# A vision block in ten token tiles of 128 rows instead of eleven of 111

## What is computed

```python
h = concat([cls, patches @ W.T + b], 1) + pos_enc          # 32 x 37 x 256, patches of 768 values
# mixer, on x = layernorm(h); cumsum runs over the tokens of one image
Z   = cumsum(x, 1) / counts                                 # counts = 1..37
a_b, a_t = (x @ Wq.T) @ V_b, (x @ Wq.T) @ V_t
c_b, c_t = cumsum((x @ Wk.T) @ W_b, 1), cumsum((x @ Wk.T) @ W_t, 1)
out = (a_b * c_b @ U_b.T + alpha * (a_t * (Z @ X_t) * c_t @ U_t.T)) / counts + bias
h   = h + out @ Wo.T
# experts, on x = layernorm(h): 8 experts, 256 -> 1024 -> 256, gelu, best two by softmax(x @ w_router + b_router)
# expert e takes its first 185 tokens in token order (cap), the rest of its tokens get nothing from it
h   = h + sum over kept choices of gate * expert_e(x) / sum of kept gates
```

## Time and profile before

| what | value |
|---|---|
| median of three runs | 164.17 us |
| profiled execution | 163.18 us |
| its span | 161.4 us |
| mean granted clock of TensorE | 0.993 |
| instructions | 3080 |

### The profile page before, as it was taken

The page is one execution under the profiler, slowest core; times in us unless marked ns, Lnnn a source line. Parts: engine busy times, 40 slices in busy tenths (PEclk is TensorE's granted clock), DMA queues, the critical chain, the costliest instruction groups (busy, mean ns, idle before and its releaser), DMA issues.

```text
span 161.4 us, 3080 instructions
## 1 busy us (share of the span) xinstructions
PE 152.6 (95%) x1033; PEld 143.7 (89%) x1033; DVE 105.6 (65%) x342; ACT 83.0 (51%) x208; POOL 53.3 (33%) x54
## 2 busy tenths in 40 slices
PE   7999999999999999989899999999999999999950
PEld 7669999978799799889889989999999999999950
DVE  0085983598477898994098858769488596694610
ACT  4125653482256979434335658366573774746200
POOL 3003550007140000121717427266183580703351
PEclk9999999999999999999999999999999999999997
DMA  5999960088005444300189985897879878710422
GB/s 174 403 418 415 403 196 0 2 295 276 0 0 140 120 131 133 85 4 0 52 255 350 314 276 84 300 262 247 254 138 314 261 203 258 177 19 4 47 24 23
DMA packets 17263, 28.47 MB, mean 176 GB/s; under 512 B 1289, under 2 KB 13875, under 8 KB 17125
## 3 DMA queue, kind: packets, MB, share of 16 engines
q1 hardware_dynamic: 14789, 25.48, 46.9%
q0 software_dynamic: 2464, 2.86, 10.3%
HBM read 24.20 MB, written 4.14 MB: 176 GB/s over the span
## 4 chain that ended last, share of the span: by engine, by line
PE 76%; DMA 10%; DVE 3%; issue 3%; POOL 2%; SPq 1%; POOLq 1%; ACT 1%; DVEq 0%
PE ps L1265 21%; PE ps L1288 10%; PE ps L1114 7%; PE ps L1169 7%; DMA w_even<-w 5%; PE ps L1094 5%; PE ps L1184 4%; PE ps L1290 4%; DMA first_t<-first 4%; PE ps L1199 3%; PE ps L1226 2%; PE ps L1298 2%; PE ps L1204 2%; DMA rows_in<-xrows,src_row 2%; PE ps L1212 1%
## 5 line engine op out<-in xcount | busy, mean ns | idle before, releaser
L498 POOL DMA_INDIRECT out_rows<-out_s,dst_row x16 | 23.8, 1486 | 38.6 <-ACT out_s L664 32.2
L640 ACT ACTIVATE first_t<-ps,b_cur 128x186 f32<-128x186 f32 x64 | 23.1, 413 | 24.7 <-PE ps L1265 24.7
L1288 PE MATMUL ps<-hid_hl,split 128*128 128x372 f32 x96 | 29.0, 369 | 0.0
L1290 PE MATMUL ps<-hid_hl,split 128*128 128x186 f32 x96 | 23.9, 249 | 0.0
L1265 PE MATMUL ps<-first_t,w_even 128*128 128x186 f32 x128 | 21.8, 322 | 0.7 <-ACT first_t L525 0.7
L1265 PE MATMUL ps<-first_t,patch_t 128*128 128x186 f32 x128 | 21.7, 322 | 0.1
L964 DVE CAST hid_hl<-first_t 128x372 fp32r<-128x372 f32 x28 | 10.9, 388 | 15.7 <-ACT first_t L640 15.7
L1265 PEld LDWEIGHTS ps<-first_t,w_even 128*128 128x128 f32 x128 | 20.1, 190 | 1.0 <-issue 1.0
L1265 PEld LDWEIGHTS ps<-first_t,patch_t 128*128 128x128 f32 x128 | 20.1, 190 | 0.4 <-issue 0.4
L483 POOL DMA_INDIRECT rows_in<-xrows,src_row x14 | 15.4, 1097 | 10.5 <-DVE src_row L934 6.5
L1290 PEld LDWEIGHTS ps<-hid_hl,split 128*128 128x128 f32 x96 | 18.3, 191 | 0.0
(11 more groups left out here) (173 smaller groups left out, 286.0 us busy)
## 6 DMA issues: line engine op xcount, KB each, us to landing
w_even<-w SPq DMA_DIRECT2D x8, 1024.0 KB, 5.8
patch_t<-w SPq DMA_DIRECT2D x8, 1024.0 KB, 5.4
patch_t<-patches SPq DMA_DIRECT2D x2, 972.0 KB, 11.7
att<-attn SPq DMA_DIRECT2D x1, 1280.0 KB, 8.9
first_t<-first SPq DMA_DIRECT2D x1, 870.0 KB, 6.5
out_rows<-h SPq DMA_DIRECT2D x3, 288.0 KB
xrows<-xn SPq DMA_DIRECT2D x3, 288.0 KB, 2.4
first_t<-first SPq DMA_DIRECT2D x1, 580.0 KB, 4.2
```

What stands on the lines that cost most here:

```text
L498: pool.indirect_dma_start(out=out[:, :], out_offset=bass.IndirectOffsetOnAxis(ap=dst_row[0:SIZES[s], c:c + 1], axis=0), in_=out_s[q][0:SIZ ...
L640: ins = act.activation(hid[:, f, :], bank(pair)[:, (f % 2) * SL:(f % 2 + 1) * SL], ACT.Gelu, bias=b1_cur[q][:, f:f + 1])
L1288: pe.matmul(dst[:, 0:2 * SL], w2_h[q][:, f, cols], hid_hl[:, f].rearrange("p a s -> p (a s)"), start=f == 0, stop=False)
L1290: ins = pe.matmul(dst[:, 0:SL], w2_l[q][:, f, cols], hid_hl[:, f, 0], start=False, stop=f == KF - 1)
```

## The change

Tiles have 128 rows, so ten of them, the last with 32; groups have 2, 3, 3 and 2 tiles. Group edges no longer fall between images: a group's patches are those of the images that its tokens reach (7, 11, 10 and 4 images instead of 9, 9, 9 and 5), and the scans start from the last column of the group before. POOL scales from a table spread over all images. `means2` goes from DVE to ACT, the router's bias is added in `rstd2`, `choose` loses its own bias, reduction and flooring ahead of the maximum. The marks carry the row in the tile, the tile's first row and a one for "taken", three parts instead of two, and `read_marks` sums the first two in one reduction. Four bridge products in front of `slots 0` go, two come in front of `slots 1`. The orders of all engines are written anew: A goes before B_ from `xn_t` on.

```diff
-TB = 3
-TT = TB * T
+TT = 128
-GROUPS = [(0, 3), (3, 3), (6, 3), (9, 2)]
+GROUPS = [(0, 2), (2, 3), (5, 3), (8, 2)]
-BRIDGES = {('slots', 0): 4, ('pick', 0): 3}
+BRIDGES = {('pick', 0): 3, ('slots', 1): 2}
-CHOICES = [(0, 6), (6, 5)]
-PATCHES = [(t0 * TB, min(B, (t0 + n) * TB)) for t0, n in GROUPS]
+CHOICES = [(0, 5), (5, 5)]
+ENDS = [0] + [min(B, -(-(t0 + n) * TT // T)) for t0, n in GROUPS]
+PATCHES = list(zip(ENDS[:-1], ENDS[1:]))
...
-    c[:, C_IDS] = np.stack([p + 1 + 0 * t, 0 * p + t], -1).reshape(128, -1)
+    c[:, C_IDS] = np.stack([p + 0 * t, 0 * p + t * TT, 1 + 0 * p + 0 * t], -1).reshape(128, -1)
...
-        UNITS = [("proj", A, 0), ("mac", 0, 1), ("uw", 0, 2), ("proj", B_, 3), ("norm1", A, 0), ("proj", C, 1),
-                 ("norm1", B_, 2), ("proj", E, 3), ("norm1", C, 0), ("xn_t", B_, 1), ("norm1", E, 2), ("xn_t", A, 3),
-                 ("zc", B_, 1), ("zc", A, 3), ("a", A, 0), ("a", B_, 2), ("xn_t", E, 1), ("xn_t", C, 3), ("y", B_, 2),
-                 ("zc", C, 1), ("norm2", B_, 3), ("y", A, 0), ("a", E, 2), ("zc", E, 1), ("norm2", A, 0), ("a", C, 1),
-                 ("y", E, 3), ("y", C, 2), ("norm2", E, 1), ("norm2", C, 3), ("slots", 0, 2), ("pick", 0, 0),
-                 ("slots", 1, 2), ("pick", 1, 0)]
+        UNITS = [("proj", A, 0), ("mac", 0, 1), ("uw", 0, 2), ("norm1", A, 0), ("proj", B_, 3), ("proj", C, 1),
+                 ("norm1", B_, 2), ("xn_t", A, 3), ("norm1", C, 0), ("proj", E, 1), ("xn_t", B_, 3), ("zc", A, 2),
+                 ("zc", B_, 1), ("a", B_, 3), ("norm1", E, 0), ("a", A, 2), ("xn_t", C, 1), ("y", A, 2), ("zc", C, 1),
+                 ("y", B_, 2), ("xn_t", E, 3), ("norm2", A, 0), ("zc", E, 3), ("norm2", B_, 1), ("a", E, 2), ("a", C, 3),
+                 ("y", E, 0), ("y", C, 2), ("norm2", E, 3), ("norm2", C, 0), ("slots", 0, 2), ("pick", 0, 1),
+                 ("slots", 1, 2), ("pick", 1, 1)]
...
         DVE_ORDER = [("proj", A), ("uw", 0), ("stats1", A), ("proj", B_), ("rstd1", A), ("proj", C), ("stats1", B_),
...
+                     ("xn_low", A), ("rstd1", B_), ("stats1", C), ("rstd1", C), ("proj", E), ("sums", A), ("sums", B_),
+                     ("prod", A), ("stats1", E), ("add_up", A), ("prod", B_), ("rstd1", E), ("sums", C), ("add_up", B_),
+                     ("sums", E), ("rstd2", A), ("prod", E), ("prod", C), ("add_up", E), ("rstd2", B_), ("add_up", C),
+                     ("choose", 0), ("rstd2", E), ("place", 0), ("count", 0), ("rstd2", C), ("choose", 1), ("below", 0),
+                     ("place", 1), ("count", 1), ("know", 0), ("know", 1)]
+        ACT_ORDER = [("mac", 0), ("m_high", 0), ("root1", A), ("norm1", A), ("xn_high", A), ("root1", B_), ("norm1", B_),
+                     ("root1", C), ("xn_copy", B_), ("norm1", C), ("xn_copy", C), ("root1", E), ("norm1", E), ("xn_copy", E),
+                     ("means2", A), ("squares2", A), ("keep2", A), ("root2", A), ("rows2", A), ("means2", B_),
+                     ("squares2", B_), ("root2", B_), ("keep2", B_), ("rows2", B_), ("means2", E), ("squares2", E),
+                     ("root2", E), ("means2", C), ("squares2", C), ("root2", C), ("rows2", E), ("rows2", C), ("keep2", C),
+                     ("keep2", E)]
...
-                pool.tensor_tensor(by_image(z_s[R:, c0:c1]), by_image(z_s[R:, c0:c1]),
-                                   per_image(slice(R, 128), (c1 - c0) // T), ALU.mult).then_inc(pool_step, 1)
+                pool.tensor_tensor(z_s[R:, c0:c1], z_run[R:, c0:c1], z_s[R:, c0:c1], ALU.mult).then_inc(pool_step, 1)
...
-                mark(pool, k, slice(0, 2), ids.rearrange("p (t c) -> p t c", c=2)).then_inc(pool_marked, 1)
+                mark(pool, k, slice(0, ID_PARTS), ids.rearrange("p (t c) -> p t c", c=ID_PARTS)).then_inc(pool_marked, 1)
...
+            pool.memset(spare[:, :], 0.0)
+
             pool.wait_ge(src_ready, 1)
             gather(1, 1)
...
                 if kind == "rstd2":
                     for r, a, b in parts:
-                        dve.tensor_tensor(logit[0:r, a:b], read_s[0:r, a:b, 0:NE],
-                                          rstd[0:r, NT + a:NT + b].rearrange("p (t a) -> p t a", a=1
-                                                                             ).broadcast_to((r, b - a, NE)), ALU.mult)
+                        for t in range(a, b):
+                            dve.scalar_tensor_tensor(logit[0:r, t], read_s[0:r, t, 0:NE], rstd[0:r, NT + t:NT + t + 1],
+                                                     b_router_s[0:r], ALU.mult, ALU.add)
...
-                step(dve.tensor_tensor(logit[:, ts], logit[:, ts],
-                                       b_router_s.rearrange("p (a e) -> p a e", a=1).broadcast_to((TT, n, NE)), ALU.add))
-                step(dve.tensor_reduce(largest[:, ts], logit[:, ts], AX.X, ALU.max))
-                step(dve.scalar_tensor_tensor(floored[:, ts], top1, FLOOR, logit[:, ts], ALU.add, ALU.max))
                 for t in tiles:
-                    ins = dve.max(top2[:, t], floored[:, t])
+                    ins = dve.max(top2[:, t], logit[:, t])
                 step(ins)
+                dve.scalar_tensor_tensor(floored[:, ts], top1, FLOOR, logit[:, ts], ALU.add, ALU.max)
+                step(dve.scalar_tensor_tensor(top2[:, ts, 1], top2[:, ts, 0], FLOOR, top2[:, ts, 1], ALU.add, ALU.max))
...
+                before, same = (0.0, 0.0), same_image[:, c0:c1]
+                if n:
+                    before = (z_run[R:, c0 - 1:c0], c_run[:, c0 - 1:c0])
+                    dve.wait_ge(z_summed, nth(DVE_ORDER, ("sums",), ("sums", n - 1)))
+                    drained(dve, "zc", n - 1)
+                dve.tensor_tensor_scan(z_run[R:, c0:c1], same[R:], p[R:, 0:w], before[0], ALU.mult, ALU.add
                                        ).then_inc(z_summed, 1)
...
-                step(dve.tensor_copy(slot_id[:, :], row))
-                n = marked(dve.scalar_tensor_tensor(slot_id[:, :], tile, float(TT), slot_id[:, :], ALU.mult, ALU.add))
-                dve.tensor_copy(coef[:, :], part[0])
-                behind(n)
-                dve.tensor_scalar(src_row[:, :], slot_id[:, :], -1.0, 0.0, ALU.add, ALU.max).then_inc(src_ready, 1)
+                with nc.allow_low_precision(reason="two whole numbers that sum to a row's number"):
+                    dve.tensor_reduce(src_row[:, :], bank(MARKS_BANK)[0:ST, 0:ID_SUM * SC].rearrange("p (c q) -> p q c", c=ID_SUM),
+                                      AX.X, ALU.add).then_inc(src_ready, 1)
```

110 lines of the change are left out of this document (50 added, 60 removed).

## The result

The changed kernel takes 164.84 us (median of 11 executions, 164.05 to 166.84) against 164.06 for the kernel before (11 executions, 163.35 to 164.35). The ratio is 1.0066, 95% interval 1.0040 to 1.0093: slower by 0.8 us in the medians and by 1.1 us by the ratio, where 1.75 us less was forecast.

What follows compares the result with a forecast made beforehand. The prediction took PE's list of matmuls before the first expert as the bound. PE time -1.7 us, waits +0.35 and marks to gather -0.4 summed to -1.75, from 164.17 to 162.4 us; range 161.1 to 163.7.

Steps and rivals of the forecast that it cites:

- The waits of the new order: Before the first expert: PE's waits for late neighbours, 0.90 us in place of 0.55, net +0.35 us.
- For choice 1 PE decides: Second choice, before `slots 1`: DVE done near 61.9 us, PE's pick 0 and bridges near 62.1, so no wait.
- the start: First loads and proj A: `att` lands earlier and mac starts at 11.0 instead of 11.76 us, -0.76 us.
- pick: PE's pick products before the experts: 44 passes become 40 at 0.165 us each, -0.66 us.
- proj B and C +1.77, proj E -0.73, norm1 -0.22: PE's projections and first norm: wider B and C add 1.77 us, narrower E saves 0.73, fewer transposes save 0.22.
- norm2, -0.58: Second norm on PE: eleven tiles become ten at 0.58 us each, -0.58 us.
- Bridges, -0.51: Covering products on PE: `slots 0` loses four, `slots 1` gains two, four passes fewer, -0.51 us.
- The opened waits, 0.9: PE's new waits at xn_t B, y C, norm2 C, `slots 0` and the like, together 0.90 us.
- Nothing, then; 0.5 us if ACT runs late: `means2` moved from DVE to ACT in the second norm: no cost expected, 0.5 us if ACT runs late.
- the order eats the saving: Rival: DVE and ACT chains in the middle open 1 us more, 163.4 us; chance 0.16.
- Marks to gather, -0.4: From the marks to the first gather: shorter lookup and reduction cut PE's wait for gathered rows, -0.4 us.
- The clock: my rival, at 0.10: Rival before the experts: PE's clock halves during waits, one 6 us interval giving 165.4 us; chance 0.10 with similar mishaps.

Runs made afterwards that it cites:

- b_copy128: The kernel before with GpSimd's copy of the scale table over all 128 partitions instead of 64; 163.52 us, ratio 0.9991.
- a_late_copy: The changed kernel with GpSimd's copy of the scale table moved behind its three m_l subtractions; 163.60 us, ratio 1.0017.
- a_same: The changed kernel, unaltered, timed and traced a second time; 165.55 us, ratio 1.0099 to the kernel before.
- l_full_last: a_late_copy with pick reading all 128 rows of the last token tile, the 96 spare ones zero; 163.01 us, ratio 0.9958.
- l_bridge4: a_late_copy with four bridge products put back in front of `slots 0`; 164.02 us, ratio 1.0043.
- a_pad512: The changed kernel with the rows of `first_t` padded from 508 to 512 columns; 165.59 us, ratio 1.0101.
- b_nobridge: The kernel before without its four bridge products in front of `slots 0`; 163.88 us, ratio 0.9989.
- a_att_alone: The changed kernel with SyncE holding back all later loads until the attention weights land; one execution, 170.54 us.

## Why the prediction was wrong, step by step

The step that failed is "The waits of the new order". It has no wait ahead of proj B, where PE came 0.95 us late because of a copy on GpSimd that I had put at nothing, and it says "For choice 1 PE decides", where PE waits some 0.5 us. Two terms of PE's list were mis-sized besides: the start (-0.76, measured -0.1) and pick (-0.66, measured about -0.1).

- **The start, -0.76.** "`att` becomes the bound and mac starts at 11.0": it became the bound (a wait of 0.66 us) but landed no earlier. The 11.76 that I compared with is the modelled end of the product before; PE's timeline has mac's first product at 11.60 before and 11.49 after, so the gain is 0.1, and even a start at 11.0 would have gained only 0.6. My bound "+0.4 if `att` doesn't move" was the case and too small: the miss is 0.65. Why `att` does not move is open.
- **Ahead of proj B: not in the sum.** The diff doubles the partitions of a copy on GpSimd and I did not price it. Doubling is not what hurt (b_copy128), but the copy now shuts VectorE out for 1 us where PE waits for the first split, and 0.95 us of that reaches proj B (a_late_copy). The earlier trace rows had shown me such a contention at the marks, and I used it only there.
- **proj B and C +1.77, proj E -0.73, norm1 -0.22.** Right. The 72 passes take 12.67 us where the clock holds (a_same), 12.5 forecast. By the Trainium skill's per-pass rule (TensorE: Matmul & The Clock Gate, "Wait — 56ns, not 53.3ns?"), with the addition taken from it as in the prediction, 12.3; by the rule alone 11.5, an estimate. The row was the better guide. proj E takes 2.94 us.
- **norm2, -0.58.** -0.3. A tile costs 0.62 us (0.27 + 0.35), not 0.58. The four router products of nine columns follow the width of their weights: 0.29 us at 32 columns, 0.37 at 74, 0.47 at 111 and 0.51 at 128 in PE's timelines.
- **pick, -0.66.** About -0.1. The number of passes is right; the last tile of 32 rows costs 0.58 us at its changes of height (l_full_last). I had taken the mean of a row without so short a tile.
- **Bridges, -0.51.** The four ahead of `slots 0` are worth 0.55 us in the changed program where the clock holds (l_bridge4), so the size is right there, but it is the price of the guard.
- **The opened waits, 0.9.** Right in the middle: y C 0.27, norm2 C 0.30, xn_t B and slots 0 under 0.1. Then 0.72 before the first expert, as before.
- **Choice 1 and ScalarE: put at nothing.** "For choice 1 PE decides" and, of ScalarE with `means2`, "Nothing, then; 0.5 us if ACT runs late". In a_pad512, without a fall, PE needs 2.11 us from the bridges ahead of `slots 1` to pick 1 (64.31 to 66.42), 0.28 of it a wait for ScalarE's copies of `h` and some for the choice; behind a fall it needs 1.57 (a_same, 65.66 to 67.23). So 0.5 us is opened, which is half of my rival "the order eats the saving". Whether it is the move of `means2`, no run tested.
- **Marks to gather, -0.4.** Right in kind and size: from expert 0's first product to the turn of the gathered rows it takes 10.77 us for 11.26, and there is no wait of PE's for the rows any more (the earlier trace rows has 0.47). GpSimd's marks take 2.33 us (forecast 2.6), and beside them VectorE's `weight` product 0.97 us for 0.76. The gather starts 0.48 us after the reduction to `src_row` starts, against 1.1 after the last of the three operations in the earlier trace rows. GpSimd had been idle for 5.7 us now and for 6.5 then, and the small fill of `spare` runs before that idle time; what shortens the start is open.

```profile
71.44 2.33 POOL L323 TENSOR_TENSOR marks<-at_q,cst 128x480 bf16<-128x480 bf16 x2 [20.49 <-DVE at_q L1008]
73.72 0.09 POOL L513 MEMSET spare<- 1x1 f32 x1
79.48 1.14 POOL L486 DMA_INDIRECT rows_in<-xrows,src_row  x1 [5.67 <-DVE src_row L937]
```

```profile
72.84 0.97 DVE L1018 TENSOR_TENSOR weight<-weight,got 128x20 f32<-128x20 f32 x1
...
79.00 0.19 DVE L937 TENSOR_REDUCE src_row<-ps 96x16 int32<-96x32 f32 x1 [1.82 <-PE ps L1083]
```

- **The clock: my rival, at 0.10.** It was to be priced at one stretch of 6 us. It came as up to two of 3.4 us, costing 1.55 and 0.9, in a part of the executions. (The rival's own sum is not of one piece: its 6 us cost 3, its ten microseconds cost 10.) I had named the waits and the missing bridges and then argued with the earlier trace rows that the kernel before stands waits of that size. That was the wrong comparison. Ahead of the second fall PE has a stretch of nine-column and 40-column products with waits of 0.27 and 0.30 us in it, and the kernel before has such a stretch only with the bridges behind it. b_nobridge shows that the bridges keep the clock up; as it has a wait of 0.96 us in their place, it does not show whether the waits or the short products bring the fall. Nor do they decide alone: from 57.8 to 61.4 us PE is busy for 3.44 us in a_same, where the clock falls, and for 3.38 in a_pad512, where it does not.

The account of the undisturbed program: -1.75 forecast, +0.65 start, +0.95 the first split, +0.3 norm2, +0.6 pick, +0.5 choice 1 and ScalarE make +1.25 us; the spans without the falls differ by 1.1. The times agree roughly: a_same's execution at 0.998 is 0.9 us above the kernel before, and the seven of the changed kernel's eleven with clocks of 0.989 or more have a mean 0.6 us above it. So most of the measured 0.8 to 1.1 us is the program, and the falls add the rest. How it divides exactly is not settled: the start varies by 1 us from execution to execution.

"It is wrong if the granted clock has a slice below 1.00 there" and "if PE waits more than 1.5 us in all between 11 and 67" were the right flags; both came true (0.49 of the 0.66, 0.70, 0.27 and 0.30 make 1.76).

## What to carry to other kernels

Price every operation that the diff makes larger, on the idle engines too, and look at what runs beside it in the first microseconds of its life: the copy on GpSimd cost nothing on its own engine and 0.95 us on another's. When tiles change size, look at the rest tile and at products with few columns; neither followed the proportion here. Where a guard of covering products goes, count the guard's price and the fall's together, and time enough executions to see the steps. To take a fall out of a trace, compare with a trace that has none: a fall hides waits, and the arithmetic of half the clock (1.7 us) overstated this one (0.9).

## What the runs showed of the hardware

- In the traces of the changed kernel a GpSimd copy and VectorE's two-input subtraction exclude each other by whole instructions: 72 columns took 1.21 us beside the copy and 0.22 without it.
- The overlap has two outcomes for nearly the same program: 1.2 us for the copy with VectorE held up, or 3.66 with VectorE at full speed. None of eight edits moved a kernel from one to the other.
- Successive fp32 passes of 186 columns stand 0.157 us apart at one height, and about 0.25 twice in a row where 128 rows follow 32 or the reverse.
- Four fp32 products of nine columns take 0.29 us with weights 32 columns wide, 0.37 with 74, 0.47 with 111 and 0.51 with 128.
- Before the experts the granted clock fell for 3.41 us at a time (once for about 6.8, in a_att_alone), and whether it does differs between executions of one program (clocks of 0.975, 0.986 and 0.998 in a_same).
- A fall costs what it does not cover: 1.7 us in the kernel before without bridges, 0.9 at the same place in the changed one, where PE would have waited.
